# A four-layer transformer kernel: the DMA of the softmax shift rows moves from SyncE's queue to ScalarE's, and the planned order is laid out anew

## The chip, the cores and the metric

The kernel runs on one core of one Trainium2 chip. The time is device microseconds of one execution, from launch to end. Before the change it is 3052.14 us, the median of 3 runs (3050.81 to 3057.52).

## What is computed

Sixteen sequences of 256 tokens with 256 features pass through four transformer layers with 16 heads of 16 features. Seven attentions come out of it: numbers 0, 2 and 4 are self attentions over 256 keys (0 and 2 causal, 4 with a mask), numbers 1, 3, 5 and 6 are cross attentions over a context of 77 rows. Layers 0 and 2 have a dense feed-forward part, layer 1 has a mixture of eight experts with two experts per token, layer 3 is a cross attention alone. Each attention is, in short:

```
q, k, v = x @ wq + bq, ctx @ wk + bk, ctx @ wv + bv       # 16 heads of 16
scores  = q @ k.T / sqrt(16)                              # masked where causal or padded
out     = softmax(scores) @ v @ wo + bo
x       = layernorm(x + out) * gain + bias
```

## The kernel before

The program has three phases. Phase "a" runs layer 0 and both attentions of layer 1 for all 16 sequences and scatters the tokens to their experts; phase "b" runs the experts in 39 groups; phase "c" gathers the experts' outputs and runs layers 2 and 3. In phases a and c up to seven sequences are in flight at once (LANES, line 45).

Nobody writes the instruction order by hand. Functions such as attend_steps (line 317) describe each piece of work as a step: its engine, its booked duration (us), how long after it its result can be used (lag), the steps that it comes after, and the buffers that it takes and gives. Plan.run (line 93) simulates the engines with these figures: whichever step can start first goes next, and among equals the more urgent. Urgency is the length of the way to the end, shifted by hand-fitted amounts for each stage in the table AHEAD (line 446). The result is one fixed list of steps per engine. The engine programs (tensor_program at 683, scalar_program at 916, sync_program at 1404 and so on) go through these lists and emit real instructions with waits on semaphores. In the real run each engine keeps its listed order, and an instruction that has to wait holds up all that is behind it on its engine or queue.

Scores are computed in a split form. Query and key values are split into three bfloat16 parts (high, middle and low, lines 940 to 951 and 1366), and SyncE copies these by DMA into stacks of six blocks of 16 partitions, "qs" for queries and "ks" for keys (copy steps, line 1430, each copy 128 KB for 256 tokens). TensorE multiplies the stacks once with queries as rows (qm steps, line 736); VectorE takes each row's maximum (line 1106) and turns it into a negative shift in three bfloat16 parts. TensorE transposes these (turn_shift, line 744), ScalarE copies them out of PSUM into the tile "shift", of 48 partitions by 256 (turned_shift, line 955), and a DMA of 24 KB puts them as three more partitions under the query stack (shift_in, line 1433, issued by SyncE). Only then can TensorE multiply the stacks again with keys as rows and the shift included (km steps, line 756, opened by the mask matmul of line 865 or 869 in self attention). ScalarE takes the exponential (exp, line 962), and TensorE multiplies with the values (pv, line 772).

There are 64 shift_in steps in phase a and 48 in phase c. The step is booked as 0.76 us of SyncE plus a lag of 2.2 us, which Plan.run multiplies by 1.35 in these phases. The shift tile is one of two buffers; ScalarE waits at line 954 until the DMA that last read it has landed.

Of the kernel before, what the change touches and what calls it, by code (L numbers as in the profile page):

```python
# [22 lines left out]
NPART = 3  # L23
STACK = 6 * HD
# [292 lines left out]
def attend_steps(plan, b, at, qs, ks, values, stacked):  # L317
    causal, n = at in CAUSAL, S if at in SELF else C
    lab = (b, at)
    maxima = ("maxima", lab)  # L320
    units = query_units(at)
    for u, (cost, _, _) in enumerate(units):
# [13 lines left out]
              bank=bank, least=least)  # L336
    plan.step("scalar", "turned_shift", b, at, us=0.41, after=[("turn_shift", b, at)], takes=["shift"], gives=["bank"],
              bank=bank, shift=shift)
    plan.step("sync", "shift_in", b, at, us=0.76, lag=2.2, after=[("turned_shift", b, at)], gives=["shift"], landing="shift",
              shift=shift, qs=qs)  # L340
    flat = ("flat", lab)
    for g in range(H // 4):
# [80 lines left out]
def start_steps(plan, loads):  # L423
# [8 lines left out]
    for at in (0, 1, 2, 3):  # L432
# [10 lines left out]
          "outs": ("out", "add"), "ffs": ("ff", "relu"), "gains": ("bias", "gain", "shift")}  # L443
STAGE_OF = {kind: stage for stage, kinds in STAGES.items() for kind in kinds}
NORM_OF = {"l0_1": 0, "l0_2": 1, "l0_3": "l0_ff", "l1_0": 2, "l1_1": 3, "l1_3": 4, "l2_1": 5, "l2_2": "l2_ff", "l2_3": 6}
AHEAD = {"a": {"enters": 0.9, ("enters", "a"): -0.6, "norms": 3.3, ("norms", 0): 126.0, ("gains", 0): -19.1,
               "turns": -0.8, ("turns", 0): 2.0, "projs": 0.8, ("projs", 0): 13.1, "values": -0.4,
               ("values", 0): 1.0, ("maxima", 0): 0.1, "shifts": 0.2, ("shifts", 0): 69.6, "scores": 0.1,
               ("scores", 0): -0.1, "pvs": -1.3, ("pvs", 0): 0.9, "ends": 0.3, ("ends", 0): 43.8,
               ("enters", 1): -1.6, ("projs", 1): -1.3, ("values", 1): -0.2, "outs": -0.8, ("outs", 0): 0.3,  # L450
               ("norms", 1): 15.5, ("gains", 1): -0.2, ("turns", 1): 9.5, ("maxima", 1): -0.1, ("shifts", 1): 132.0,
               ("scores", 1): 0.1, ("pvs", 1): 230.3, ("ends", 1): -0.4, ("outs", 1): 34.4,
               ("norms", "l0_ff"): -0.5, ("gains", "l0_ff"): 16.9, "ffs": -0.4, ("ffs", "l0_ff"): 1.3,
               ("outs", "l0_ff"): 0.1, ("gains", 2): 20.1, ("projs", 2): -0.1, ("shifts", 2): 1.0,
               ("scores", 2): 0.3, ("pvs", 2): 1.6, ("ends", 2): 0.2, ("enters", 3): -0.6, ("projs", 3): -0.3,
               ("outs", 2): 152.6, ("norms", 3): 74.0, ("turns", 3): -0.1, ("maxima", 3): 1.6, ("shifts", 3): 0.6,
               ("pvs", 3): 1.3, ("ends", 3): -0.8, ("outs", 3): -0.1, ("norms", "l1_2"): -0.5,
               ("turns", "l1_2"): 0.2, ("gains", "l1_2"): 1.8},
         "c": {"enters": 2.3, "norms": 8.4, ("norms", 4): -9.6, "turns": 1.2, ("turns", 4): -0.2, "gains": 4.7,
               ("gains", 4): 30.5, "projs": 0.7, ("projs", 4): -0.5, "values": -0.4, ("values", 4): 1.4,  # L460
               "maxima": -0.2, "shifts": 102.7, ("shifts", 4): 20.1, "scores": 0.2, ("scores", 4): 28.6,
               "pvs": -0.2, ("pvs", 4): 0.1, "ends": -0.1, ("ends", 4): -48.7, ("enters", 5): 2.2,
               ("projs", 5): 67.2, ("values", 5): 15.0, "outs": -1.0, ("outs", 4): 0.4, ("norms", 5): -269.4,
               ("turns", 5): 2.9, ("gains", 5): -88.8, ("maxima", 5): -0.3, ("shifts", 5): 86.2,
               ("scores", 5): -0.5, ("pvs", 5): 16.5, ("ends", 5): 11.0, ("outs", 5): 9.0, ("norms", "l2_ff"): -4.7,
               ("turns", "l2_ff"): 18.2, ("gains", "l2_ff"): 5.1, "ffs": 36.7, ("ffs", "l2_ff"): 30.1,
               ("outs", "l2_ff"): 38.3, ("enters", 6): 1.1, ("projs", 6): 77.4, ("values", 6): 121.8,
               ("norms", 6): 4.9, ("turns", 6): -1.6, ("gains", 6): 4.8, ("shifts", 6): 2.8, ("scores", 6): 19.9,
               ("pvs", 6): 129.6, ("ends", 6): -12.2, ("outs", 6): 29.6, ("norms", "l3"): -8.7,
               ("gains", "l3"): 14.4}}  # L470


def ahead_of(phase):
# [442 lines left out]
def scalar_program(act, k, phase):  # L916
# [4 lines left out]
    for s in k.plan.order[phase]["scalar"]:  # L921
# [18 lines left out]
        elif s.kind == "high":  # L940
            bank, parts, n = tile(s, "bank"), tile(s, "parts"), C if s.part == "c" else S
            bias = k.biases[at][0 if s.part == "q" else 1]
            until.wait_ge(*done("proj", b, at, s.part))
            until.wait_ge(*freed(s, "parts"))
            for m in range(KT):
                ins = act.activation(parts[:, 0, m, 0:n], bank[:, 0, m * n:(m + 1) * n], ACT.Identity, bias=bias[:, m:m + 1])
            ins.then_inc(k.own(s), 1)
        elif s.kind == "middle":
            parts, rest, n = tile(s, "parts"), tile(s, "rest"), C if s.part == "c" else S
            until.wait_ge(*done("rest", b, at, s.part))  # L950
            act.activation(parts[:, 1, :, 0:n], rest[:, :, 0:n], ACT.Copy).then_inc(k.own(s), 1)  # L951
        elif s.kind == "turned_shift":
            until.wait_ge(*done("turn_shift", b, at))
            until.wait_ge(*freed(s, "shift"))
            act.activation(tile(s, "shift"), tile(s, "bank")[0:NPART * H, 0, 0:S], ACT.Copy).then_inc(k.own(s), 1)
        elif s.kind == "exp":
            bank, prob, (g, u) = tile(s, "bank"), tile(s, "prob"), s.part
            rows, (_, _, (first, cols)) = C if at in CROSS else P, key_units(at, g)[u]
            until.wait_ge(*done("km", b, at, s.part))
            if u == 0:  # L960
                until.wait_ge(*freed(s, "prob"))
            act.activation(prob[0:rows, first:first + cols], bank[0:rows, 0, 0:cols], ACT.Exp, scale=SCALE).then_inc(k.own(s), 1)  # L962
        elif s.kind == "value":
            bank, values = tile(s, "bank"), tile(s, "values")
            keys, n = (P, QT) if at in SELF else (C, 1)
            until.wait_ge(*done("value_proj", b, at))
            until.wait_ge(*freed(s, "values"))
            act.activation(values[0:keys, 0:n, 0:H, 0:HD],
                           bank[0:keys, 0, 0:n * D].rearrange("p (t h d) -> p t h d", h=H, d=HD), ACT.Copy).then_inc(k.own(s), 1)
        elif s.kind == "relu":  # L970
            bank, hidden = tile(s, "bank"), as_hidden(tile(s, "hidden"))
            until.wait_ge(*done("ff", b, at, s.part))
            if s.part == 0:
                until.wait_ge(*freed(s, "hidden"))
            for j in range(2):
                f = 2 * s.part + j
                ins = act.activation(hidden[:, f, :], bank[:, 0, j * S:(j + 1) * S], ACT.Relu, bias=k.ff[at][2][:, f:f + 1])
            ins.then_inc(k.own(s), 1)
        elif s.kind == "gelu":
            bank, hidden, b1 = tile(s, "bank"), tile(s, "hidden"), tile(s, "b1")  # L980
            until.wait_ge(*done("expert", b, "b", s.part))
            until.wait_ge(*done("b1_load", b, "b"))
            if s.part == 0:
                until.wait_ge(*freed(s, "hidden"))
            n = ROWS_OF[b]
            per_bank = 2 * S // n
            for j in range(per_bank):
                f = per_bank * s.part + j
                ins = act.activation(hidden[:, f, 0:n], bank[:, 0, j * n:(j + 1) * n], ACT.Gelu, bias=b1[:, f:f + 1])  # L989
            ins.then_inc(k.own(s), 1)  # L990
        elif s.kind == "route_exp":
            r = tile(s, "r")
            until.wait_ge(*done("logit_less", b, at))
            act.activation(r["prob"], r["logit"], ACT.Exp).then_inc(k.own(s), 1)
        elif s.kind == "gap_exp":
            r = tile(s, "r")
            until.wait_ge(*done("gap", b, at))
            act.activation(r["e2"], r["gap"], ACT.Exp).then_inc(k.own(s), 1)
        elif s.kind == "group_store":
            n, slot = ROWS_OF[b], SLOTS[b]  # L1000
            first = slot * GROUP if slot < PAIRS else PAIRS * GROUP + (slot - PAIRS) * HALF
            until.wait_ge(*done("group_sum", b, "b"))
            act.dma_start(rows_of(k.sorted_flat, slice(first, first + n)), tile(s, "y")[:, 0:n // P, :]).then_inc(k.own(s), 16)
        else:
            raise ValueError(s.kind)
# [398 lines left out]
def sync_program(sp, k, phase):  # L1404
# [3 lines left out]
    for s in k.plan.order[phase]["sync"]:  # L1408
# [10 lines left out]
        elif s.kind == "copy":  # L1419
# [8 lines left out]
                until.wait_ge(*done("low", b, at, role))  # L1428
            for block in COPIES[role == "q"][part]:
                sp.dma_start(stack[block * HD:(block + 1) * HD, :, :], parts[:, part, :, 0:n]).then_inc(k.own(s), 16)  # L1430
        elif s.kind == "shift_in":
            until.wait_ge(*done("turned_shift", b, at))
            sp.dma_start(tile(s, "qs")[STACK:STACK + NPART, :, :], tile(s, "shift")).then_inc(k.own(s), 16)
        elif s.kind == "clear":
            rows = lambda first, n: (k.sorted_in[first, :].rearrange("(q p) d -> p q d", p=P),
                                     k.zeros.unsqueeze(1).broadcast_to([P, n // P, D]))
# [368 lines left out]
```

## Time and profile before

| | us |
|---|---|
| median of 3 runs | 3052.14 |
| lowest and highest | 3050.81, 3057.52 |
| the profiled execution, whole | 3048.22 |
| its span, first to last instruction | 3045.8 |
| TensorE busy, share of the span | 2830.4, 93% |
| VectorE busy | 1681.8, 55% |
| ScalarE busy | 1331.7, 44% |
| GpSimd busy | 986.7, 32% |

Phase a goes from the start to about 1410 us, phase b from about 1424 to 1951, phase c from there to the end. Instructions that only issue a DMA are not counted as busy; they stand in the timeline with a q behind the engine's name (SPq, ACTq). "idle before <-releaser" is the time that an engine stood still before an instruction and what ended it. The mean granted TensorE clock over the span is 0.964 of full speed.

### The profile page before, as it was taken

To read this page: it belongs to the slowest core of one execution; us is meant where nothing else is said; L and a number is where in the kernel's file an instruction comes from. 1 tells how busy PE (TensorE), PEld (TensorE's weight loads), DVE (VectorE), ACT (ScalarE), POOL (GpSimd) and SP (SyncE) were. 2 spreads that over 40 slices of the span, in tenths; PEclk is the share of its full clock that TensorE was granted. 3 is DMA by queue.
4 is the path that set the end of the run, shared out by engine and by line. 5 is a ranking of instruction groups with operands and counts; after the bars stand their busy time and mean duration, and the time that the engine had idled before them with its cause. 6 is when DMAs were issued, how large, how long until landed. Compare 5 with 4: busy or idle time off the path is not lost. (4 is left out here: it accounts for less than half of the span.)

```text
span 3045.8 us, 58500 instructions
## 1 busy us (share of the span) xinstructions
PE 2830.4 (93%) x22574; PEld 2279.3 (75%) x22574; DVE 1681.8 (55%) x4086; ACT 1331.7 (44%) x2955; POOL 986.7 (32%) x1103
## 2 busy tenths in 40 slices
PE   6989999989999989975999999889999999999996
PEld 4768888768888777754888888656777777777774
DVE  4646556776755867554110010276676766767664
ACT  2535445556455455332222222245455545555442
POOL 2313224444323444322000000252344444444343
PEclk8999999999999999986999999899999999999997
DMA  9755546585664674754767766375466555666342
GB/s 141 119 72 67 63 54 89 84 114 75 75 71 59 90 98 72 190 74 135 241 225 231 224 211 220 87 111 63 53 85 76 80 79 75 82 77 78 43 50 40
DMA packets 393627, 317.68 MB, mean 104 GB/s; under 512 B 152155, under 2 KB 377307, under 8 KB 393339
## 3 DMA queue, kind: packets, MB, share of 16 engines
q1 hardware_dynamic: 370994, 276.25, 54.6%
q0 software_dynamic: 8272, 23.73, 2.8%
q10 hardware_dynamic: 14085, 13.97, 1.7%
q8 instruction: 179, 2.93, 0.5%
q14 instruction: 97, 0.79, 0.1%
HBM read 133.54 MB, written 36.57 MB: 56 GB/s over the span
## 5 line engine op out<-in xcount | busy, mean ns | idle before, releaser
L962 ACT ACTIVATE a_prob<-a_bank 128x512 f32<-128x512 f32 (+1 forms) x640 | 332.8, 603 | 146.5 <-PE a_bank L756 142.9
L1106 DVE TENSOR_REDUCE a_maxima<-a_bank 128x2 f32<-128x512 f32 (+3 forms) x576 | 339.2, 644 | 82.7 <-PE a_bank L736 82.0
L962 ACT ACTIVATE c_prob<-c_bank 128x512 f32<-128x512 f32 (+1 forms) x512 | 266.3, 599 | 194.7 <-PE c_bank L756 194.4
L989 ACT ACTIVATE b_group_hidden<-b_bank,b_b 128x256 f32<-128x256 f32 (+1 forms) x312 | 123.3, 452 | 387.7 <-PE b_bank L820 387.7
L1106 DVE TENSOR_REDUCE c_maxima<-c_bank 128x6 f32<-128x462 f32 (+1 forms) x448 | 260.4, 635 | 45.2 <-PE c_bank L736 43.9
L865 PE MATMUL a_bank<-a_causal_b,keep_identb 128*128 128x256 bf16 (+1 forms) x768 | 243.1, 316 | 29.9 <-DMA a_qs<-a_shift 12.9
L820 PE MATMUL b_bank<-b_group_xt,b_w 128*128 128x256 f32 (+1 forms) x1248 | 261.6, 364 | 6.3 <-DVE b_group_xt L1157 6.3
L802 PE MATMUL b_bank<-b_w,b_group_hidden 128*128 128x256 f32 x1136 | 251.7, 380 | 0.9 <-ACT b_group_hidden L989 0.9
L820 PEld LDWEIGHTS b_bank<-b_group_xt,b_w 128*128 128x128 f32 x1248 | 220.6, 192 | 33.7 <-DVE b_group_xt L1157 8.3
L802 PEld LDWEIGHTS b_bank<-b_w,b_group_hidden 128*128 128x128 f32 x1136 | 215.6, 190 | 29.7 <-ACT b_group_hidden L989 1.3
L1163 DVE TENSOR_TENSOR b_group_y<-b_bank,b_b 128x512 f32<-128x512 f32 (+1 forms) x39 | 25.1, 644 | 336.1 <-PE b_bank L802 336.1
L1359 POOL TENSOR_TENSOR c_tok<-c_tok,weights_row_L_xattn_ln_g 128x512 f32<-128x512 f32 x64 | 81.2, 1268 | 192.9 <-PE c_bank L705 192.7
L756 PE MATMUL a_bank<-a_qs,a_ks 99*128 99x128 bf16 x1536 | 143.5, 222 | 0.0
L736 PE MATMUL a_bank<-a_ks,a_qs 96*128 96x128 bf16 x1536 | 142.4, 220 | 0.0
L756 PEld LDWEIGHTS a_bank<-a_qs,a_ks 99*128 99x128 bf16 x1536 | 121.6, 99 | 22.9 <-issue 1.4
L736 PEld LDWEIGHTS a_bank<-a_ks,a_qs 96*128 96x128 bf16 x1536 | 120.2, 98 | 23.6 <-issue 2.2
L1132 DVE STREAM_TRANSPOSE a_flat<-a_bank 128x512 f32<-128x512 f32 x128 | 90.0, 708 | 86.5 <-PE a_bank L772 86.0
L714 PE MATMUL a_bank<-a_xt,a_at_q 128*128 128x256 f32 x512 | 131.8, 404 | 5.7 <-ACT a_xt L935 4.4
L802 PE MATMUL a_bank<-a_at_o,a_heads 128*128 128x256 f32 x512 | 131.3, 402 | 5.6 <-DVE a_heads L1140 5.4
L1152 DVE TENSOR_TENSOR a_tok<-a_bank,a_tok 128x512 f32<-128x512 f32 x80 | 54.8, 687 | 146.3 <-PE a_bank L802 146.0
L1369 POOL TENSOR_TENSOR a_parts_q<-a_rest,a_parts_q 128x512 bf16<-128x512 f32 x64 | 74.0, 1158 | 183.0 <-ACT a_parts_q L951 183.0
L1386 POOL DMA_INDIRECT c_pair_y<-sorted_out,keep_rows x64 | 62.8, 982 | 200.7 <-issue 195.1
(255 smaller groups left out, 6224.0 us busy)
## 6 DMA issues: line engine op xcount, KB each, us to landing
b_w<-in_L_xattn_e_w SPq DMA_DIRECT2D x78, 1024.0 KB, 7.4
a_qs<-a_parts_q SPq DMA_DIRECT2D x384, 128.0 KB
c_qs<-c_parts_q SPq DMA_DIRECT2D x288, 128.0 KB
a_ks<-a_parts_k SPq DMA_DIRECT2D x192, 128.0 KB, 5.9
c_ks<-c_parts_k SPq DMA_DIRECT2D x96, 128.0 KB, 5.5
sorted_in<-a_zeros SPq DMA_DIRECT2D x8, 1024.0 KB
b_group_x<-sorted_in SPq DMA_DIRECT2D x32, 256.0 KB, 6.8
sorted_out<-b_group_y ACTq DMA_DIRECT2D x32, 256.0 KB, 4.8
```

The costliest lines, as they stand in the source:

```text
L714: ins = pe.matmul(bank[:, 0, m * n:(m + 1) * n], weight[:, kt, m * P:(m + 1) * P], xt[:, kt, 0:n], start=(kt == 0), stop=(kt == KT - 1))
L736: ins = pe.matmul(bank[:, 0, to:to + m], qs[0:STACK, h, q * P:(q + 1) * P], ks[0:STACK, h, kt * P:kt * P + m], start=(at in CROSS), stop=( ...
L756: ins = pe.matmul(bank[0:kn, 0, to:to + m], ks[0:STACK + NPART, h, kt * P:kt * P + kn], qs[0:STACK + NPART, h, q0:q0 + m], start=(at in CR ...
L802: ins = pe.matmul(bank[:, 0, q * D:(q + 1) * D], heads[:, kt, q * P:(q + 1) * P], weight[:, kt, :], start=(kt == 0), stop=(kt == kts - 1))
L820: ins = pe.matmul(bank[:, 0, j * n:(j + 1) * n], weight[:, kt, f * P:(f + 1) * P], xt[:, kt, 0:n], start=(kt == 0), stop=(kt == KT - 1))
L865: pe.matmul(blocks, k.identb, k.causal[:, keys_first, :].unsqueeze(1).broadcast_to([P, 4 // step, P]), start=True, stop=False)
L962: act.activation(prob[0:rows, first:first + cols], bank[0:rows, 0, 0:cols], ACT.Exp, scale=SCALE).then_inc(k.own(s), 1)
L989: ins = act.activation(hidden[:, f, 0:n], bank[:, 0, j * n:(j + 1) * n], ACT.Gelu, bias=b1[:, f:f + 1])
L1106: v.tensor_reduce(maxima[:, q:q + qn, h:h + n].rearrange("p q h -> p h q"), bank[:, 0, 0:cols].rearrange("p (j q n) -> p j q n", j=n, q=qn ...
L1132: v.transpose(flat, tile(s, "bank")[:, 0, :].rearrange("p (g b c) -> p g b c", g=2, c=32)).then_inc(k.own(s), 1)
L1359: pool.tensor_tensor(x, x, over(k.gains[at][0]), ALU.mult).then_inc(k.own(s), 1)
L1369: pool.tensor_tensor(parts[:, 2, :, 0:n], rest[:, :, 0:n], parts[:, 1, :, 0:n], ALU.subtract).then_inc(k.own(s), 1)
```

## The change

The step shift_in is planned and issued on ScalarE, with 0.1 us booked where SyncE had 0.76. ScalarE waits for the end of its own copy and then issues the same DMA with the same semaphore. The table AHEAD has new values in both phases, so the planned order of all engines is laid out anew. Nothing that is computed changes.

```diff
-    plan.step("sync", "shift_in", b, at, us=0.76, lag=2.2, after=[("turned_shift", b, at)], gives=["shift"], landing="shift",
+    plan.step("scalar", "shift_in", b, at, us=0.1, lag=2.2, after=[("turned_shift", b, at)], gives=["shift"], landing="shift",
               shift=shift, qs=qs)
...
-AHEAD = {"a": {"enters": 0.9, ("enters", "a"): -0.6, "norms": 3.3, ("norms", 0): 126.0, ("gains", 0): -19.1,
...
+AHEAD = {"a": {"enters": 0.9, ("enters", "a"): -2.7, "norms": 1.6, ("norms", 0): 201.3, "gains": -7.4,
...
             act.activation(tile(s, "shift"), tile(s, "bank")[0:NPART * H, 0, 0:S], ACT.Copy).then_inc(k.own(s), 1)
+        elif s.kind == "shift_in":
+            until.wait_ge(*done("turned_shift", b, at))
+            act.dma_start(tile(s, "qs")[STACK:STACK + NPART, :, :], tile(s, "shift")).then_inc(k.own(s), 16)
...
-        elif s.kind == "shift_in":
-            until.wait_ge(*done("turned_shift", b, at))
-            sp.dma_start(tile(s, "qs")[STACK:STACK + NPART, :, :], tile(s, "shift")).then_inc(k.own(s), 16)
```

## Rows read from the trace of the kernel before

**Rows 1.** The page: busy us, share of the span, instructions of each engine.
```profile
PE 2830.4 (93%) x22574; PEld 2279.3 (75%) x22574; DVE 1681.8 (55%) x4086; ACT 1331.7 (44%) x2955; POOL 986.7 (32%) x1103
```

**Rows 2.** By stretch: length, busy of PE, PEld, DVE, ACT, POOL; clock; DMA share; GB/s.
```profile
1350.00:1450.00 100.00, 61.66 (x361) 47.34 (x360) 44.87 (x171) 22.32 (x49) 31.90 (x34) 0.68 0.47 133
2060.00:2800.00 740.00, 717.50 (x5676) 542.47 (x5675) 500.83 (x1147) 383.01 (x833) 321.26 (x355) 1.00 0.59 75
2950.00:3046.00 96.00, 69.58 (x485) 53.01 (x483) 45.59 (x106) 29.20 (x64) 32.70 (x37) 0.78 0.20 35
```

**Rows 3.** Waits of TensorE (us, times, longest); the first is the same for 2060 to 2800.
```profile
PE c_bank L869 <- DMA c_qs<-c_shift: 20.9, 13, 3.5
PE a_bank L865 <- DMA a_qs<-a_shift: 12.9, 6, 5.9
PE a_bank L865 <- DMA a_qs<-a_parts_q: 10.7, 3, 7.7
PE a_bank L756 <- DMA a_qs<-a_shift: 9.4, 6, 3.6
PE a_bank L714 <- ACT a_xt L935: 4.4, 4, 1.1
PE c_bank L756 <- DMA c_qs<-c_shift: 2.0, 2, 1.8
```

**Rows 4.** SyncE's timeline, the chain (start, us, what), TensorE's timeline, at 2521 to 2537.
```profile
2520.98 1.89 SPq L1430 DMA_DIRECT2D c_qs<-c_parts_q  x3
...
2531.14 5.61 DMA c_qs<-c_shift
...
2536.80 0.39 PE L869 MATMUL c_bank<-c_weights_mask_k,keep_identb 128*128 128x512 bf16 x1 [0.88 <-DMA c_qs<-c_shift]
```

**Rows 5.** Timeline of SyncE and TensorE at 1369 to 1373.
```profile
1369.69 0.77 SPq L1433 DMA_DIRECT2D a_qs<-a_shift  x1
1372.47 1.29 PE L756 MATMUL a_bank<-a_qs,a_ctx_ks 99*77 99x256 bf16 x5 [1.14 <-DMA a_qs<-a_shift]
```

**Rows 6.** Timeline of ScalarE and SyncE at 1261 to 1270.
```profile
1261.61 0.37 ACT L955 ACTIVATE a_shift<-a_bank 48x256 bf16<-48x256 f32 x1
1268.31 1.99 SPq L1433 DMA_DIRECT2D a_qs<-a_shift  x1
```

**Rows 7.** Instructions of line 1433: duration ns min/median/max, first and last start.
```profile
L1433 SPq DMA_DIRECT2D c_qs<-c_shift x48: 737/767/784, 2012.7 to 3014.7; - x48
```

**Rows 8.** Waits of SyncE's queue: total us, times, longest us.
```profile
SPq L1433 <- ACT c_shift L955: 297.0, 42, 15.9
```

**Rows 9.** DMA issues of the expert phase: count, KB each, median us to landing.
```profile
b_group_x<-sorted_in SPq DMA_DIRECT2D x32, 256.0 KB, 6.8
sorted_out<-b_group_y ACTq DMA_DIRECT2D x32, 256.0 KB, 4.8
```

**Rows 10.** Issues of the ones rows on ScalarE (line 925) and SyncE (1412).
```profile
L925 ACTq DMA_DIRECT2D a_ctx_ks<-in_ones_b x3: 716/720/865, 1.6 to 3.3; - x3
L1412 SPq DMA_DIRECT2D c_ctx_ks<-in_ones_b x2: 731/792/852, 1952.0 to 1952.9; - x2
```

**Rows 11.** Timeline of ScalarE behind three shift copies, and one row of TensorE.
```profile
2532.52 0.84 ACT L946 ACTIVATE c_parts_q<-c_bank,keep_columns 128x256 bf16<-128x256 f32 x2 [1.41 <-PE c_bank L714]
...
2554.20 0.84 ACT L946 ACTIVATE c_parts_q<-c_bank,keep_columns 128x256 bf16<-128x256 f32 x2 [1.30 <-PE c_bank L714]
...
2579.25 0.38 ACT L968 ACTIVATE c_ctx_values<-c_bank 77x256 f32<-77x256 f32 x1 [0.50 <-PE c_bank L723]
2579.69 1.02 ACT L935 ACTIVATE c_xt<-c_bank,keep_columns 128x256 f32<-128x256 f32 x2
2580.80 1.96 PE L714 MATMUL c_bank<-c_xt,c_weights_at_q 128*128 128x256 f32 x8
```

**Rows 12.** Timeline of ScalarE at a shift copy of phase a.
```profile
487.16 0.37 ACT L955 ACTIVATE a_shift<-a_bank 48x256 bf16<-48x256 f32 x1
487.42 3.94 ACT L962 ACTIVATE a_prob<-a_bank 77x512 f32<-77x512 f32 x8
```

More of the change, by code:

```diff
@@ L445 @@
 NORM_OF = {"l0_1": 0, "l0_2": 1, "l0_3": "l0_ff", "l1_0": 2, "l1_1": 3, "l1_3": 4, "l2_1": 5, "l2_2": "l2_ff", "l2_3": 6}
-AHEAD = {"a": {"enters": 0.9, ("enters", "a"): -0.6, "norms": 3.3, ("norms", 0): 126.0, ("gains", 0): -19.1,
[L447 to L470, printed above, removed]
@@ new lines @@
+AHEAD = {"a": {"enters": 0.9, ("enters", "a"): -2.7, "norms": 1.6, ("norms", 0): 201.3, "gains": -7.4,
+               ("gains", 0): 65.6, ("turns", 0): -0.4, "projs": 0.8, ("projs", 0): 35.2, "values": -0.3,
+               ("values", 0): 0.3, ("maxima", 0): 11.1, "shifts": 1.1, ("shifts", 0): 88.2, "scores": 0.1,
+               ("scores", 0): -0.8, "pvs": -1.3, ("pvs", 0): 0.3, "ends": 1.7, ("ends", 0): 121.4,
+               ("enters", 1): 17.2, ("projs", 1): -1.4, ("values", 1): -1.2, "outs": -1.5, ("outs", 0): 1.3,
+               ("norms", 1): 51.4, ("gains", 1): -4.6, ("turns", 1): 57.5, ("shifts", 1): 25.3, ("scores", 1): 0.1,
+               ("pvs", 1): 336.2, ("ends", 1): -1.3, ("outs", 1): 44.9, ("norms", "l0_ff"): 10.2,
+               ("gains", "l0_ff"): 53.9, ("turns", "l0_ff"): -0.5, "ffs": -0.2, ("outs", "l0_ff"): -28.8,
+               ("turns", 2): 93.3, ("values", 2): 3.3, ("maxima", 2): 0.3, ("shifts", 2): 125.4, ("scores", 2): 0.3,
+               ("pvs", 2): -99.3, ("ends", 2): -39.3, ("enters", 3): -4.6, ("values", 3): 2.1, ("outs", 2): 163.5,
+               ("norms", 3): 84.9, ("turns", 3): -0.1, ("gains", 3): 14.8, ("shifts", 3): 2.7, ("pvs", 3): 0.9,
+               ("ends", 3): -5.1, ("outs", 3): 0.2, ("norms", "l1_2"): -0.5, ("turns", "l1_2"): 0.6,
+               ("gains", "l1_2"): 23.0},
+         "c": {"enters": 16.0, ("enters", "c"): -4.4, "norms": 123.0, ("norms", 4): -0.3, "turns": 0.5,
+               ("turns", 4): -0.9, "gains": -37.5, ("gains", 4): 6.6, "projs": 32.9, ("projs", 4): 9.0,
+               "values": -1.6, ("values", 4): 2.4, "maxima": -0.2, "shifts": 425.5, ("shifts", 4): -3.8,
+               "scores": -16.5, ("scores", 4): 220.9, "pvs": -14.9, ("pvs", 4): 54.2, "ends": -77.9,
+               ("ends", 4): 1.2, ("enters", 5): 3.3, ("projs", 5): 74.2, ("values", 5): 107.5, "outs": -1.2,
+               ("outs", 4): 0.4, ("norms", 5): -397.8, ("turns", 5): 69.3, ("gains", 5): -47.6, ("maxima", 5): -0.1,
+               ("scores", 5): 37.9, ("pvs", 5): 241.4, ("ends", 5): 160.2, ("outs", 5): 245.1,
+               ("norms", "l2_ff"): 14.3, ("turns", "l2_ff"): 88.8, "ffs": 65.1, ("ffs", "l2_ff"): -11.4,
+               ("outs", "l2_ff"): 47.3, ("enters", 6): 2.4, ("projs", 6): 107.5, ("values", 6): 132.2,
+               ("norms", 6): -7.9, ("turns", 6): 0.8, ("gains", 6): 7.2, ("shifts", 6): 2.7, ("scores", 6): 58.8,
+               ("pvs", 6): 47.1, ("ends", 6): -0.5, ("outs", 6): 57.1, ("norms", "l3"): -3.2,
+               ("gains", "l3"): -21.4}}
```

## The prediction

> **What bounds the kernel now.** I read the page's busy table first: TensorE is busy 2830.4 of 3045.8 us, ScalarE 1331.7 [rows 1]. So the end is set by TensorE's work plus its idle time, 3045.8 − 2830.4 = 215 us, and an edit that leaves TensorE's work alone can only move that idle time. The table by stretch then says where it lies: from 2060 to 2800 only 22.5 us are lost, but 38.3 us in the hundred at 1350 and 26.4 us in the last 96 [rows 2]. In the steady stretch the granted clock is 1.00, the upper of the two levels (2.4 GHz), so nothing is to be had there from the clock. The waits of TensorE name the causes: the landing of the shift rows costs 20.9 + 12.9 + 9.4 + 2.0 = 45.2 us, in 13 + 6 + 6 + 2 = 27 waits, the copies of query parts 10.7 us, and the largest wait for ScalarE 4.4 us in all [rows 3]. The 20.9 us lie all between 2060 and 2800 and are nearly the whole of the 22.5 [rows 2, 3]. The change aims at the largest single wait of the steady stretch.
>
> Next, why that wait is there. In the pattern that recurs every 63 us, SyncE issues 12 copies back to back from 2520.98 on, and behind them the shift rows at 2531.14; the chain shows 5.61 us to the landing, and TensorE stands 0.88 us [rows 4]. Where nothing has been issued for a while (1369.69) TensorE starts on the shift at 1372.47, so that landing took 2.7 us [rows 5]. The transfer is the same, so about 3 us of the landing are what stands before it in SyncE's queue. And at 1261.98 the copy on ScalarE ends, but SyncE issues the rows only at 1268.31 [rows 6], behind clears and stack copies of its own; that is the longest wait, 5.9 us [rows 3].
>
> **The change part by part.** *The issue leaves SyncE.* 64 + 48 = 112 issues of 0.77 us, 86 us of SyncE [rows 7], and, more important, the waits in which SyncE stood with a shift issue at its head, in the last phase alone 297.0 us [rows 8]. Copies behind it can go earlier. Of the 10.7 us of waits for copies I take nothing back for that: 7.7 us is a single wait [rows 3]. Bounds 0 and −11.
>
> *The landing gets shorter.* On ScalarE's queue nothing stands ahead of the rows in the two attention phases, apart from the first loads. No row of the kernel before shows this transfer on that queue while copies run. Nearest rows: the empty case, 2.7 us [rows 5], and the 256 KB store from ScalarE's queue in the expert phase, beside SyncE's loads, 4.8 us against 6.8 for a load of that size from SyncE [rows 9]. The rows are 24 KB, a tenth, so I take the middle of 2.7 and 4.8, some 3.8 us; the bounds are 2.7 and the present 5.6. The cover that TensorE's order gives is landing less wait, 5.61 − 0.88 = 4.7 us [rows 4]; at 3.8 us that wait is gone. Over the 27 waits this leaves, by my estimate, some 5 us: where the landing is at 2.7 already (the 1.14 us at 1372.47, [rows 5]) or the cover is under 3.8. Gain 45 − 5 = 40 us; with the landing unchanged it is 0.
>
> The Trainium skill speaks on both sides here ("DMA: Bandwidth & Descriptors"). Against, in "SWDGE vs HWDGE vs iDMA": transfers of all issuing engines run on the same 16 DMA engines, and another issuer saves only issue time. By it the landing would stay near 6 us and the 40 us would be 0. For, in "Queues, rings and completion order": each DMA engine takes turns between the queues it has work for, by packets; by that the rows pass the copies. That ScalarE's store lands before SyncE's load would [rows 9] agrees rather with the second.
>
> *The issue lands on ScalarE.* The planner books 0.1 us for it. Its real price: loads of the ones rows, also to three partitions, take 720 ns on ScalarE and 792 on SyncE at the median [rows 10], so the issuer matters little, and I take SyncE's 0.77 us for the shift [rows 7]. ScalarE must first wait for the end of its own copy, which loses the overlap of 0.1 us seen at 487.16 + 0.37 against 487.42 [rows 12]. So 0.87 us each, 112 × 0.87 = 97 us. ScalarE is busy 383.0 of 740 us in the steady stretch [rows 2], so most of it lies beside TensorE's work. Queued behind it are exp, the parts' high and middle, the turned tokens and the values; pv, projections and free banks on TensorE wait for these. Three shift copies make up a sequence of the last phase. Behind the first (2531) ScalarE idles 1.41 us: no cost. Behind the second (2552) comes one exp, then 1.30 us idle: no cost. Behind the third (2578) the values begin 0.50 us later, the turned tokens end at 2580.71, and TensorE's projection on them begins at 2580.80 [rows 11]; pushed by 0.87 − 0.50 = 0.37 us, with 0.1 us of slack, TensorE loses 0.3 us. One in three loses 0.3: 112 × 0.1 = 11 us. In the first phase a run of eight exps without a gap [rows 12] passes the whole push on, and the new order counts on 0.1 us, so I take half as much again: 16 us lost. Bounds 0 and 97.
>
> *The order.* The steps' priorities are new, so TensorE's own order changes in both phases. Its work does not: the same matmuls. What can move is the idle time at the starts and ends of the phases, such as the 38.3 and 26.4 us [rows 2]. No row says which way; I take 0, and ±12 us, a fifth of those 65.
>
> **Sum.** The profiled execution took 3048.2 us, of which 3045.8 are span; the median of three runs is 3052.1, so 4 us above. −40 + 16 + 0 = −24: profiled 3024, median 3028 us.
>
> **Rivals.** *1. ScalarE passes the price on.* The order books 0.1 us where 0.77 is real, and puts dependent work close behind. It decides from the point where more than 40/0.87 = 46 of the 112 issues reach TensorE in full. For it: the exps without a gap [rows 12]. Against: ScalarE is half idle [rows 2], and its longest wait in rows 3 is 1.1 us. With two thirds, 3052 − 40 + 65 = 3077; with all, 3109. Slower. *2. The landing does not shorten*, because the 16 DMA engines, busy 0.59 of the stretch [rows 2], are the same for both queues: gain 0, cost 11 to 16, so 3063 to 3068. Slower; the first rule of the Trainium skill above is this case. Against: the 4.8 us [rows 9]. *3. The waits go but the time comes back*, at the next late thing or at the phase ends of a changed order (twice the ±12 above): 3046 to 3058, no change. *4. The change does not do what it says*: if the planner sets other ScalarE steps between the copy and the issue, the rows start later by an exp or more, 0.5 us each (3.94 us for eight, [rows 12]); with 2 us on most waits half the gain is gone, 3046 to 3050, no change.
>
> **How the numbers follow.** A measurement of this kernel tells about 0.2%, 6 us, from no change. Forecast (below 3046): 0.62, of which 0.05 lies under 3000. Rivals 3 and 4: 0.16. Rival 2: 0.08. Rival 1: 0.14, a third of it under 3068. The range 3000 to 3068 leaves out the 0.05 below and two thirds of rival 1, 0.09, above. The forecast's own range: landing gain 30 to 45, ScalarE 5 to 30, order ±12 give about 3000 to 3046. Faster 0.62, same 0.16, slower 0.22.
>
> **What would show it.** TensorE's waits for the shift landing fall from 45 us to under 10. The shift lands about 3.8 us after its issue on ScalarE beside copies (rival 2: 6). The issue takes 0.77 us there, and TensorE's waits for ScalarE grow by some 16 us (rival 1: over 40). SyncE's waits for the shift copy vanish. TensorE's busy time stays at 2830 ± 5 and the steady clock at 1.00. The prediction is wrong if the idle time at the phase ends moves by more than 12 us, or if TensorE's busy time moves.

## The result and the profile after

| | us |
|---|---|
| kernel before, median of 4 runs (lowest to highest) | 3051.47 (3048.48 to 3057.52) |
| kernel after, median of 4 runs (lowest to highest) | 3142.71 (3141.66 to 3144.36) |
| after / before, 95% interval | 1.0297 (1.0279 to 1.0315) |

The change makes the kernel 3.0% slower, 91 us. The forecast was 3028 us, faster; the range ended at 3068. In the code of after, every line from 956 on stands 3 lower than in before (the issue on ScalarE is L958, the exp L965, the stack copies stay L1433).

The page of after: span and busy times; they answer to [rows 1].

```profile
span 3140.9 us, 58466 instructions
...
PE 2857.0 (91%) x22492; PEld 2288.4 (73%) x22574; DVE 1675.9 (53%) x4086; ACT 1336.2 (43%) x2955; POOL 986.6 (31%) x1103
```

The span grew by 3140.9 − 3045.8 = 95.1 us. TensorE is busy 2857.0 − 2830.4 = 26.6 us more and idle (3140.9 − 2857.0) − 215.4 = 68.5 us more. 82 matmul records are missing from this trace (22492 against 22574); at the mean of 2857.0 / 22492 = 0.127 us some 10 us of the idle time are in truth busy time, so the split is rather 58 and 37. The matmuls are the same, so the busy time can only have grown by slower ones. Where the time went is told by the same stretches in both kernels. First phase a, from the start; then phase c in three pieces, cut at its first norm, at the second and the tenth store of its results, and at the last. Columns: length; busy of PE, PEld, DVE, ACT, POOL; clock; DMA share; GB/s. Before:

```profile
0.00:1397.00 1397.00, 1288.00 (x12095) 1049.57 (x12096) 889.30 (x2260) 676.37 (x1483) 479.17 (x536) 0.96 0.61 88
1962.80:2302.10 339.30, 313.61 (x2359) 227.76 (x2362) 226.23 (x500) 164.60 (x349) 146.90 (x160) 0.96 0.63 80
2302.10:2811.18 509.08, 496.11 (x3960) 378.36 (x3956) 353.29 (x816) 263.64 (x577) 238.45 (x265) 1.00 0.60 78
2811.18:3040.30 229.12, 205.14 (x1578) 159.23 (x1570) 134.87 (x306) 99.01 (x223) 84.33 (x96) 0.92 0.35 47
```

After:

```profile
0.00:1434.00 1434.00, 1301.79 (x12096) 1048.97 (x12097) 887.90 (x2260) 678.84 (x1483) 479.52 (x536) 0.96 0.60 86
1998.90:2359.20 360.30, 317.32 (x2327) 229.99 (x2359) 223.10 (x502) 165.17 (x353) 146.08 (x160) 0.94 0.60 76
2359.20:2892.50 533.30, 502.58 (x3904) 383.81 (x3944) 358.74 (x816) 265.41 (x576) 237.64 (x264) 0.97 0.61 75
2892.50:3135.40 242.90, 210.70 (x1586) 163.26 (x1590) 128.74 (x308) 99.98 (x223) 85.87 (x98) 0.92 0.31 44
```

Phase a is 37 us longer, the ramp of phase c 21, its steady part 24, its drain 14; phase b is not longer. Read the clock of the steady part: 1.00 before, 0.97 after. TensorE's busy time there is 6.5 us more in the rows, and with the 56 missing records at 0.127 us some 14. As much, 13.8 us, is phase a's, where the clock is 0.96 in both rows.

TensorE's waits of after (total us, times, longest); the rows on the shift answer to [rows 3].

```profile
PE c_bank L756 <- DMA c_qs<-c_shift: 51.0, 15, 10.0
PE a_bank L756 <- DMA a_qs<-a_shift: 20.1, 8, 5.0
...
PE a_bank L865 <- DMA a_qs<-a_parts_q: 17.5, 6, 9.2
...
PE a_bank L744 <- DVE a_least_parts L1128: 11.6, 8, 3.9
...
PE c_bank L714 <- ACT c_xt L935: 7.1, 5, 2.9
PE a_bank L865 <- DMA a_qs<-a_shift: 6.5, 4, 2.5
```

The waits for the shift, which were to fall from 45.2 us to under 10, rose to 51.0 + 20.1 + 6.5 = 77.6 us. The issue and the chain of after say why; these rows answer to [rows 7] and [rows 4].

```profile
L958 ACTq DMA_DIRECT2D c_qs<-c_shift x48: 728/729/764, 2052.9 to 3109.7; - x48
```

```profile
2467.37 7.87 DMA c_qs<-c_shift
...
2535.62 7.81 DMA c_qs<-c_shift
```

The issue costs what was thought, 0.73 us. But the rows, alone on ScalarE's queue, take 7.8 us to land, where they took 5.61 us behind twelve copies on SyncE's queue. Over all of the steady part the chains have ten such landings in after, 7.1 to 8.0 us, and nine in before, 5.6 to 7.1 with a median of 6.35: the row of [rows 4] is the shortest of them. SyncE's timeline of after around 2535 us shows what is under way meanwhile:

```profile
2525.92 1.86 SPq L1433 DMA_DIRECT2D c_qs<-c_parts_q  x3
...
2527.86 4.13 SPq L1433 DMA_DIRECT2D c_ks<-c_parts_k  x5
...
2532.04 1.25 SPq L1433 DMA_DIRECT2D c_qs<-c_parts_q  x2
...
2533.63 0.55 SPq L1433 DMA_DIRECT2D c_ks<-c_parts_k  x1
...
2534.23 0.59 SPq L1433 DMA_DIRECT2D c_qs<-c_parts_q  x1
...
2534.93 3.23 SPq L1433 DMA_DIRECT2D c_ctx_ks<-c_parts_k  x5
```

SyncE issues copies with hardly a gap from 2525.92 to 2538.16. Twelve of 128 KB go out in 8.9 us, where before took 10.2 us for its twelve [rows 4], and five smaller ones, of 38.5 KB, follow; ScalarE's 24 KB goes out at 2535.62, behind the twelve and the first of the five.

### The profile page after: what moved, and what is told of

It reads as the page before. It is cut to its first block and busy times, and to the rows that moved or that the text cites. A ratio compares the mean times of both kernels' runs of the same rounds, so it can differ in the third digit from the quotient of the medians.

```text
span 3140.9 us, 58466 instructions
## 1 busy us (share of the span) xinstructions
PE 2857.0 (91%) x22492; PEld 2288.4 (73%) x22574; DVE 1675.9 (53%) x4086; ACT 1336.2 (43%) x2955; POOL 986.6 (31%) x1103
## 5 line engine op out<-in xcount | busy, mean ns | idle before, releaser
L965 ACT ACTIVATE a_prob<-a_bank 128x512 f32<-128x512 f32 (+1 forms) x640 | 334.1, 605 | 180.8 <-PE a_bank L756 167.8
L965 ACT ACTIVATE c_prob<-c_bank 128x512 f32<-128x512 f32 (+1 forms) x512 | 265.4, 604 | 186.3 <-PE c_bank L756 184.5
L1109 DVE TENSOR_REDUCE c_maxima<-c_bank 128x6 f32<-128x462 f32 (+2 forms) x448 | 263.3, 635 | 53.1 <-PE c_bank L736 52.7
L865 PE MATMUL a_bank<-a_causal_b,keep_identb 128*128 128x256 bf16 (+1 forms) x768 | 247.8, 323 | 38.2 <-DMA a_qs<-a_parts_q 17.5
L756 PE MATMUL c_bank<-c_qs,c_ks 99*128 99x256 bf16 x512 | 104.7, 287 | 47.5 <-DMA c_qs<-c_shift 42.3
L756 PE MATMUL a_bank<-a_qs,a_ks 99*128 99x128 bf16 x1536 | 144.1, 222 | 0.0
L756 PEld LDWEIGHTS a_bank<-a_qs,a_ks 99*128 99x128 bf16 x1536 | 121.6, 99 | 23.2 <-issue 1.6
```

Of the source, the lines that this page charges most:

```text
L756: ins = pe.matmul(bank[0:kn, 0, to:to + m], ks[0:STACK + NPART, h, kt * P:kt * P + kn], qs[0:STACK + NPART, h, q0:q0 + m], start=(at in CR ...
L865: pe.matmul(blocks, k.identb, k.causal[:, keys_first, :].unsqueeze(1).broadcast_to([P, 4 // step, P]), start=True, stop=False)
L1109: v.tensor_reduce(maxima[:, q:q + qn, h:h + n].rearrange("p q h -> p h q"), bank[:, 0, 0:cols].rearrange("p (j q n) -> p j q n", j=n, q=qn ...
```

## The experiments

The theory after the first look: **T1**, the landing depends on the copies issued before it, from whichever queue, and the new order puts more of them before the rows; the order loses the time, the queue is nearly indifferent. Rivals: **T2**, ScalarE's issue and its wait are what costs; **T3**, the new order is longer by its own dependencies, backlog or not. Times are medians; each ratio is against the kernel before on the same chip, since that kernel's median itself was 3073.7 us on the chip of e1, e2, e3 and e5 and 3049.7 to 3050.5 on the others. There is no trace of the kernel before from the slower chip, so a row of e1 or e2 beside one of before compares two chips as well.

### e1 and e2: queue alone, order alone

e1 keeps the order of before and lets ScalarE send the rows right behind its copy:

```diff
             act.activation(tile(s, "shift"), tile(s, "bank")[0:NPART * H, 0, 0:S], ACT.Copy).then_inc(k.own(s), 1)
+            until.wait_ge(*done("turned_shift", b, at))
+            send = k.plan.steps["shift_in", b, at, 0]
+            act.dma_start(tile(send, "qs")[STACK:STACK + NPART, :, :], tile(send, "shift")).then_inc(k.own(send), 16)
...
-            until.wait_ge(*done("turned_shift", b, at))
-            sp.dma_start(tile(s, "qs")[STACK:STACK + NPART, :, :], tile(s, "shift")).then_inc(k.own(s), 16)
+            pass
```

> The planned order of the kernel before on every engine, to the letter; only the issue of the shift rows moves: ScalarE sends them right behind its copy. Theory O (the loss comes from the newly laid out order, the queue itself helps or is neutral): 3020 to 3055 us, waits of TensorE on the shift landing 45 us or less. Theory Q (the loss comes from the queue: ScalarE's issue time and a landing that is no shorter): 3100 to 3150 us, most of the 91 us. In the last phase the landing of the shift issued near 2531 us tells whether ScalarE's queue passes the copies: 3.8 us if it does, 5.6 to 6.3 us if it does not.

e2 takes the order of after and lets SyncE send, at the place in its list that the planned start of the step gives:

```diff
+        sends = [s for s in order.get("scalar", []) if s.kind == "shift_in"]
+        order["sync"] = sorted(order["sync"] + sends, key=at_time)
...
-            until.wait_ge(*done("turned_shift", b, at))
-            act.dma_start(tile(s, "qs")[STACK:STACK + NPART, :, :], tile(s, "shift")).then_inc(k.own(s), 16)
+            pass
```

> The order of the changed kernel on every engine, but SyncE sends the shift rows, at the place in its list where the plan has the step in time. Theory O: 3110 to 3150 us, near the changed kernel, with a period of about 68 us per sequence in the last phase and a clock of 0.95 there. Theory Q: 3045 to 3070 us.

| | us | ratio to before (95%) |
|---|---|---|
| e1, queue alone | 3066.8 | 0.9975 (0.9960 to 0.9991) |
| e2, order alone | 3187.0 | 1.0370 (1.0343 to 1.0396) |

The order does all of the harm and the queue a little good. In the new order the queue brings somewhat more (from 1.0370 to 1.0297) than in the old one. T2 falls with this: e2, which issues nothing on ScalarE, is slower than after. On the scale where before takes 3052 us e1 is at 3044, inside what its order theory expected, and e2 at 3165, above the 3110 to 3150 expected. The chain of e1 first, then that of e2: start, us, the landing on which TensorE waited.

```profile
2485.00 6.04 DMA c_qs<-c_shift
...
2548.31 6.13 DMA c_qs<-c_shift
```

```profile
2427.78 7.73 DMA c_qs<-c_shift
...
2496.49 7.67 DMA c_qs<-c_shift
```

These are all four cases. Over the steady part, in the old order the landing takes 5.6 to 7.1 us from SyncE (before) and 5.9 to 7.0 from ScalarE (e1); in the new order 6.8 to 7.8 from SyncE (e2) and 7.1 to 8.0 from ScalarE (after). The queue doesn't shorten it. TensorE's waits of e1:

```profile
PE c_bank L756 <- DMA c_qs<-c_shift: 21.1, 12, 2.6
...
PE a_bank L865 <- DMA a_qs<-a_parts_q: 18.5, 5, 15.2
...
PE a_bank L756 <- DMA a_qs<-a_shift: 3.2, 3, 1.4
...
PE a_bank L865 <- DMA a_qs<-a_shift: 2.1, 2, 1.6
```

In phase c the wait is as before (21.1 against 20.9 + 2.0 us), with the copies still in front. In phase a, where SyncE could come late to the issue [rows 6], it falls from 12.9 + 9.4 us to 3.2 + 2.1. Part of that comes back in one longer wait for the query parts (18.5 us against 10.7). That e1's small gain is this difference fits these rows; it isn't shown by itself.

### e3: the new issue with the old priorities

The kernel after with the table AHEAD of before.

```diff
-AHEAD = {"a": {"enters": 0.9, ("enters", "a"): -2.7, "norms": 1.6, ("norms", 0): 201.3, "gains": -7.4,
...
+AHEAD = {"a": {"enters": 0.9, ("enters", "a"): -0.6, "norms": 3.3, ("norms", 0): 126.0, ("gains", 0): -19.1,
...
```

> The changed kernel with the old priority table: step moved and booked at 0.1 us on ScalarE, order planned anew from the old numbers. If any order that the planner makes from these bookings is as good as another (the small-change view of the prediction, plus or minus 12 us), 3010 to 3060 us. If an order is only as good as the fit of the table to exactly these bookings (theory O), well over the changed kernel: the planner's own end of the phases is 59 us later in the first and 94 us later in the last phase than for the kernel before, so 3180 to 3300 us.

3299.9 us, 1.0735 (1.0712 to 1.0758). The two parts of the diff can't be judged apart by swapping the table: it is fitted to the booked times, and with 0.1 us booked for the shift in place of 0.76 it lays out an order that loses 226 us. By its ratio that is 3276 us where before takes 3052, inside the 3180 to 3300 expected. This run separates nothing between T1 and T3; it shows only how much hangs on the fit of the table to the booked times, and that "order 0 ± 12 us" had no ground.

### e5: more issues on ScalarE

The kernel before, with one DMA more on ScalarE behind each shift copy (48 rows of a constant to spare DRAM), its result used by nobody.

```diff
+            until.wait_ge(*done("turned_shift", b, at))
+            act.dma_start(k.spare_rows[k.spare_sent], k.identb[0:NPART * H, :]).then_inc(k.sem("spare"), 16)
+            k.spare_sent += 1
```

> The kernel before, with SyncE still sending the shift rows, and an extra DMA issue of the same form on ScalarE behind each shift copy (48 rows of 256 bytes from a constant to spare rows in device memory; nothing else reads them). It measures what 112 issues cost on ScalarE alone. Forecast's term: 11 us, 3055 to 3070 us. Rival 1: half or more of 97 us, 3100 to 3150 us.

3080.4 us, 1.0022 (1.0010 to 1.0034): the 112 waits and issues cost 6.7 us in all, 0.06 us each, at the low end of what was expected. But they are shorter than the issue that they stand for:

```profile
L958 ACTq DMA_DIRECT2D spare_rows<-keep_identb x112: 308/309/386, 60.7 to 3047.7; - x112
```

The shift issue takes 0.73 us on ScalarE, this one 0.31, so 6.7 us is less than the price of the real one. e11 below gives that price.

### e6 and e7: both kernels with a smaller backlog

From the sixth sequence on, each copy of key parts to the stack moves one eighth of its bytes, in after (e6) and in before (e7). The attention of these sequences is therefore not that of the reference; the instructions and their order are as they were. The key copies of the first five sequences and all query copies keep their size. The edit of either:

```diff
-                sp.dma_start(stack[block * HD:(block + 1) * HD, :, :], parts[:, part, :, 0:n]).then_inc(k.own(s), 16)
+                if role == "q" or b < 5:
+                    sp.dma_start(stack[block * HD:(block + 1) * HD, :, :], parts[:, part, :, 0:n]).then_inc(k.own(s), 16)
+                else:
+                    sp.dma_start(stack[block * HD:(block + 1) * HD, 0:KT, :], parts[0:P:P // HD, part, :, 0:n]).then_inc(k.own(s), 16)
```

> The changed kernel, but from the sixth sequence on each copy of key parts into the key stack moves only the first two heads (an eighth of the bytes, the same number of issues; the rest of the stack keeps older data, so attention is not computed as in the reference). Theory B (a backlog of copies in the DMA engines, ahead of the shift rows on whichever queue they are sent, makes the landing long; TensorE's stall then also costs clock): the landing in the recurring pattern falls from 7.8 us to 3 to 5 us, the stall from 3.5 us to under 1 us, the granted clock there from 0.95 to 1.00 and the period from 68.2 to 62 to 64 us, so 3060 to 3095 us. Rival P (the new order itself holds TensorE up by its dependencies, whatever the DMAs do): period stays over 66 us, 3120 to 3140 us.

> The same cut in the kernel before (SyncE sends the shift rows; from the sixth sequence on key copies move an eighth of the bytes). Theory B: landing of the shift behind the copies falls from 6.2 us to 3 to 4.5 us, its waits in the last phase from 20.9 us to under 8, period 63.3 to about 62 us; 3025 to 3040 us on the scale where the kernel before takes 3052, so the distance between the two kernels shrinks from 91 us to 30 to 60. Rival P: the distance stays near 90 us.

| | us | ratio to before (95%) |
|---|---|---|
| e6, new order, short key copies | 3047.2 | 0.9984 (0.9967 to 1.0001) |
| e7, old order, short key copies | 2991.1 | 0.9805 (0.9786 to 0.9824) |

The bytes taken away cost the new order 3142.7 − 3047.2 = 95.5 us and the old one some 3049.7 − 2991.1 = 58.6 us. Both runs came out faster than expected, the distance between them within the 30 to 60 us expected. So the new order loses 37 us more to these bytes, and 3047.2 − 2991.1 = 56 us of the loss stay. T1 is right in kind and explains two fifths. For the rest T3 is likely but not shown: the ramps of both phases are those of the first five sequences, whose copies are whole. TensorE's waits for the shift are 26.0 us in e6 and 21.9 in e7, so the long landing itself is little of the 56. The steady part of phase c, from 2400 to 2800 us, in after, e6 and e7, in this order:

```profile
2400.00:2800.00 400.00, 376.38 (x2890) 286.80 (x2924) 265.67 (x603) 197.58 (x427) 178.02 (x198) 0.97 0.60 74
```

```profile
2400.00:2800.00 400.00, 399.05 (x3195) 303.96 (x3193) 289.95 (x663) 216.48 (x471) 193.20 (x215) 1.00 0.39 63
```

```profile
2400.00:2800.00 400.00, 399.90 (x3172) 305.39 (x3171) 284.55 (x657) 210.85 (x462) 184.08 (x206) 1.00 0.32 58
```

With short copies TensorE loses at most 1 us of 400 in either order, and the clock of the new order is back at 1.00. In the steady part, then, backlog and clock are nearly the whole loss. The 56 us lie elsewhere, as the norms of phase c (line 1084 in e6, 1081 in e7; count, duration ns, first and last start) show, e6 first:

```profile
L1084 DVE BATCH_NORM_AGGREGATE c_moments<-c_stats x160: 138/150/183, 1954.8 to 3038.5; 128x2 f32<-128x6 f32 x160
```

```profile
L1081 DVE BATCH_NORM_AGGREGATE c_moments<-c_stats x160: 123/152/183, 1928.8 to 2980.0; 128x2 f32<-128x6 f32 x160
```

Phase c begins 26 us later, so that much was lost before it, in phase a if phase b is again no longer; from first to last norm it takes 1083.7 against 1051.2 us, 32 more, with a steady part as quick: ramp and drain. What the time went into, by the sums of all rows of e6 against e7: waits for VectorE 78.0 against 69.8 us, for ScalarE 25.0 against 16.6, for the query parts 11.1 against 2.9, for the shift 26.0 against 21.9, and busy time 2845.2 against 2824.0 for the same 22574 matmuls.

### e8: the rows on GpSimd's queue

The order of before, the issue merged into GpSimd's list at its planned time.

```diff
+        sends = [s for s in order["sync"] if s.kind == "shift_in"]
+        order["gpsimd"] = sorted(order["gpsimd"] + sends, key=at_time)
...
+            pool.dma_start(tile(s, "qs")[STACK:STACK + NPART, :, :], tile(s, "shift")).then_inc(k.own(s), 16)
```

> The order of the kernel before on the other engines; GpSimd sends the shift rows, at the place in its list where the plan has the step in time. It tells whether any queue passes the backlog. Theory B1 (one line of descriptors for SyncE and ScalarE, none for GpSimd's queue): landing in the recurring pattern well under 6 us from the start of the data, though GpSimd takes about 1 us to issue and stands in its own order; 3040 to 3080 us. Theory B2 (the 16 DMA engines are simply full): landing 6 us or more, 3060 to 3120 us.

3075.5 us, 1.0086 (1.0054 to 1.0117), from two runs. Its chain shows a third queue with the same landing, 5.0 to 6.9 us over the steady part (median 6.56), so not the short one of its theory B1. Why the kernel is 0.9% slower than before is open.

```profile
2547.56 6.54 DMA c_qs<-c_shift
```

### e9: hold the copies back, on SyncE's queue

If what counts is what was issued just before, the cure is not another queue but another place in the same one. e9 is the kernel before. After planning, each shift issue in SyncE's list is moved ahead of the stack copies in front of it, as long as such a copy started at most 5 us before it in the plan and its first reader starts over 7.5 us after it, plus 0.65 us for each issue passed.

```diff
+            while (first and queue[first - 1].kind == "copy" and begun[key(queue[first - 1])] > at - window
+                   and needed[key(queue[first - 1])] > at + landing + 0.65 * (i - first)):
+                first -= 1
+            moved += i - first
+            queue[first:i + 1] = [s] + queue[first:i]
```

> The kernel before; only SyncE's list is rearranged: each issue of shift rows is moved ahead of stack copies planned in the 5 us before it, where the plan leaves these copies at least 7.5 us more than they need (162 places moved in all). SyncE then holds those copies until the shift rows are on their way; the computation is whole. Theory B (the backlog of copies ahead of the shift rows makes their landing long): in the recurring pattern the landing falls from 6.2 us to about 3 us, the waits on it from 45 us to under 20, the period from 63.3 to about 61.7 us; 3015 to 3040 us against 3052. Rival H (holding the copies only moves the wait to them): waits for stack copies grow by as much as the shift's fall, 3045 to 3070 us.

3012.5 us, 0.9863 (0.9830 to 0.9897): 38 us faster than before, 130 faster than after, with the whole computation, and just below the range expected. (The rule passes 110 copies, 52 of them in phase a, and not the 162 of the expectation.) SyncE's and TensorE's timeline of e9:

```profile
2442.80 0.76 SPq L1460 DMA_DIRECT2D c_qs<-c_shift  x1
2443.60 1.45 SPq L1457 DMA_DIRECT2D c_ks<-c_parts_k  x2
...
2447.64 0.39 PE L783 MATMUL c_bank<-c_qs,c_ks 99*128 99x256 bf16 x2
```

(Lines of e9 from TensorE's on stand 27 higher: L783 is L756, L892 is L865.) The copies now start behind the rows, and the first matmul on the rows starts 4.8 us after their issue without a wait. That bounds the landing from above; the 3 us expected can't be read, since nothing waited for it. TensorE's waits of e9 for the shift:

```profile
PE a_bank L892 <- DMA a_qs<-a_shift: 6.7, 2, 5.8
...
PE a_bank L783 <- DMA a_qs<-a_shift: 1.6, 2, 1.1
...
PE c_bank L783 <- DMA c_qs<-c_shift: 0.6, 1, 0.6
```

8.9 us of the 45.2 are left. This is the gain that the prediction computed, 36 us of waits and 38 us of time, got by another means: the place in the queue, not another queue. That waits for the copies would grow by as much (rival H) didn't happen: those for the parts are 16.8 us in all rows, against 13.8 before.

### e10 and e11: the same rule in the new order, and with ScalarE's queue

e10 is e2 with the rule of e9. e11 is e1 with the rule of e9.

```diff
-        self.order[phase] = order
+        self.order[phase] = self.shifts_first(order, begun, needs) if phase != "b" else order
```

> The same rearrangement of SyncE's list in the order of the changed kernel, with SyncE sending the shift rows (so it is to be held against order alone, 1.037 of the kernel before). Theory B: the recurring period falls from 68.6 us to 62 to 63, the granted clock there from 0.95 to 1.00; 1.005 to 1.02 of the kernel before. Rival P (the order itself is slow): 1.03 or more.

> The rearranged list of SyncE in the order of the kernel before, but ScalarE sends the shift rows; SyncE only waits for ScalarE's copy at that place and then goes on with the held copies. With the backlog gone from both, it tells what ScalarE's queue itself is worth. Theory B: the queue gives no shorter landing and costs ScalarE's issue time (ratio 1.002 measured for it), and spares SyncE 0.77 us each: within 0.3% of the run with the shift first, so 0.984 to 0.990 of the kernel before. If ScalarE's queue had a merit of its own in the landing: 0.980 or less.

| | us | ratio to before (95%) |
|---|---|---|
| e10, new order, SyncE, copies held | 3092.3 | 1.0121 (1.0093 to 1.0149) |
| e11, old order, ScalarE, copies held | 3028.7 | 0.9930 (0.9914 to 0.9945) |

In the new order the rule brings 1.0370 down to 1.0121, as expected, but the new order still stands 3092.3 − 3012.5 = 80 us above the old one. That isn't the order without the backlog either. TensorE's waits of e10 for the shift:

```profile
PE c_bank L786 <- DMA c_qs<-c_shift: 26.2, 13, 10.4
PE a_bank L786 <- DMA a_qs<-a_shift: 20.7, 6, 6.7
PE a_bank L895 <- DMA a_qs<-a_shift: 16.1, 2, 15.8
```

63.0 us of them are left, where e9 has 8.9, and in its steady part the landing still takes 6.6 to 7.8 us. So up to 54 of the 80 us are waits for the shift that the rule did not take away. One period of e10's steady part, then one of e9's:

```profile
2411.51:2474.02 62.51, 61.15 (x488) 46.97 (x493) 44.74 (x102) 33.29 (x72) 29.75 (x34) 1.00 0.65 80
```

```profile
2403.79:2465.42 61.63, 61.19 (x496) 47.23 (x498) 44.21 (x102) 32.98 (x73) 29.86 (x33) 1.00 0.62 81
```

The period is 0.9 us longer, where after's eight periods were 24.2 / 8 = 3.0 us longer each, and the clock is 1.00. Again the rest is at the ends. In the old order, with the rows no longer waiting, ScalarE's queue is a loss: e11 is 16 us slower than e9 by the medians, more than expected (0.984 to 0.990); by the two intervals it is 5 us at least. In its trace the shift waits are down as well, but the one for the query parts stands at 18.2 us where e9 has 10.7:

```profile
PE a_bank L892 <- DMA a_qs<-a_parts_q: 18.2, 4, 15.4
```

All rows of waits for ScalarE together are 23.6 us against 16.4 in e9. These 7.5 and 7.2 us make 15 of the 16. The same wait of 15 us was in e1. This is the price of the real issue of 0.73 us where the landing has nothing left to gain: 16 us for 112, 0.14 us each.

## Why the prediction was wrong

**What bounds the kernel: right.** The shift waits of 45.2 us were the largest thing to be had; e9 took 36 us of them and the kernel became 38 us faster. That some 3 us of the landing are what had been issued before it was right too, by e9; the row read for it, 5.61 us [rows 4], is the shortest of nine, whose median is 6.35.

**"The landing gets shorter", −40 us: this step failed.** It held the copies to be in the way because they stood ahead *in the same queue*. Over the steady part e1 shows 5.9 to 7.0 us on ScalarE's queue, e8 5.0 to 6.9 on GpSimd's, against 5.6 to 7.1 on SyncE's; in after, where 3.8 us was forecast, it is 7.1 to 8.0. The nearest row chosen, the 256 KB store at 4.8 us [rows 9], was a poor one: it doesn't tell what was under way beside the store, and the landing hangs on that. The Trainium skill's rule in "DMA: Bandwidth & Descriptors", section "SWDGE vs HWDGE vs iDMA", that all issuers share the 16 engines, is what these landings bear out. The rule of the same page in "Queues, rings and completion order", that an engine takes turns between queues, didn't help these rows: on a queue of their own they gained nothing. The gain that e1 does have, 8 us of time by its ratio, probably came from the other effect, the issue that no longer waits for its turn in SyncE's list: phase a's waits fell by some 17 us. The prediction had named that effect [rows 6] and given it no term.

**"The issue lands on ScalarE", +16 us: borne out.** One issue takes 0.73 us as expected, and e11 against e9 puts the whole at 16 us by the medians, with wide intervals. That it fits to the microsecond is luck: the sum of one issue in three at 0.3 us was not tested, and half of the 16 us came by way of the query parts, which it doesn't hold. In after, all rows of TensorE's waits for ScalarE grew from 14.8 to 28.8 us, as much as forecast; but e2, with no issue on ScalarE, has 30.9, so that growth belongs to the order. The 40 us of rival 1 aren't there.

**"The order", 0 ± 12 us: this step failed, and it is the large one.** e2 measures it as +3.7%, 113 us, nine times the bound. Two things were missing. The bound was made from the idle time at two places [rows 2], as if an order could only shift what is there; and no thought was given to what a new order does *to the landing*, although that had just been found to hang on the copies in front. Of the 91 us of after, 37 are lost to the backlog and its consequences (e6, e7); the other 56 lie in phase a, in the ramp and in the drain of phase c (e6 against e7). In after as a whole TensorE waits 82.1 us for VectorE in all rows, against 72.2, and 17.5 for the query parts at the opening of self attention in phase a, against 10.7 [rows 3]. Which steps of the order make them late is not settled; no run moved single steps, and none took the whole backlog away.

**The clock: not foreseen.** "Steady clock at 1.00" held for before and fell for after. The stretches behind a stall of 3.58 us in after:

```profile
2407.40:2411.00 3.60, 3.56 (x13) 2.16 (x13) 0.58 (x2) 2.12 (x4) 0.00 (x0) 0.50 1.16 122
2411.00:2414.00 3.00, 3.00 (x14) 2.31 (x13) 0.48 (x1) 0.63 (x2) 0.00 (x0) 0.70 1.00 96
2414.00:2417.00 3.00, 3.00 (x23) 2.01 (x21) 2.52 (x10) 2.19 (x6) 1.46 (x4) 1.00 0.04 9
```

TensorE is busy all of the time from 2407.4 on, but at 0.50 (1.2 GHz) it gets through 13 matmuls in 3.6 us, then 14 in 3.0, where at 1.00 (2.4 GHz) it does 23 (of a somewhat different mix). By the clock, 3.6 × 0.50 + 3.0 × 0.30 = 2.7 us are lost beside the 3.6 of the stall. But not every such stall does this. Two neighbouring periods of after have the same stall, and one of them keeps its clock; the two stalls in TensorE's timeline, and the two periods:

```profile
2612.11 0.64 PE L756 MATMUL c_bank<-c_qs,c_ks 99*128 99x256 bf16 x2 [3.50 <-DMA c_qs<-c_shift]
2680.68 0.38 PE L756 MATMUL c_bank<-c_qs,c_ks 99*128 99x256 bf16 x2 [3.56 <-DMA c_qs<-c_shift]
```

```profile
2563.94:2632.19 68.25, 64.24 (x496) 48.79 (x498) 44.85 (x102) 33.37 (x73) 29.77 (x34) 0.95 0.60 73
2632.19:2698.07 65.88, 61.55 (x496) 47.24 (x498) 44.83 (x102) 33.03 (x73) 29.75 (x34) 1.00 0.62 76
```

The slow clock alone makes the period 2.4 us longer, with as many matmuls in it. Nor is before free of it: behind its stall of 2.33 us the clock is at 0.50 too, behind the one of 2.58 us at 2220.86 it stays at 1.00.

```profile
2600.94 0.39 PE L869 MATMUL c_bank<-c_weights_mask_k,keep_identb 128*128 128x512 bf16 x1 [2.33 <-DMA c_qs<-c_shift]
```

So a stall can cost 2.4 to 2.7 us more than its length, and its length alone doesn't tell which will. Over the eight steady periods a clock of 0.97 is 533 × 0.03 = 16 us, close to the 14 us of busy time more. Of the backlog's 37 us, waits for the shift are some 28: with the short copies they fall from 77.6 to 26.0 us in the new order and from 45.2 to 21.9 in the old one. The slow work behind them was not separated by a run.

**The rivals.** The answer is none of the four. Rival 2's premise held, the landing doesn't shorten; but e1, which is that case in the old order, came out at 0.9975 and not 11 to 16 us slower, and after is 91 us slower. Rival 1 gave 3077 to 3109, on the right side, by a mechanism that e2 excludes: there ScalarE issues nothing, and the time is longer still. Rival 3 was closest in kind, the time coming back at the ends of a changed order, and gave 3046 to 3058.

**What would show it.** Of the signs named, the issue price came as foreseen (0.73 us) and SyncE no longer waits for the shift copy; the landing came out as in rival 2 or worse (7.8 us), shift waits rose, busy time rose by 26.6 us and the steady clock fell to 0.97. The last line, "wrong if the idle time at the phase ends moves by more than 12 us, or if TensorE's busy time moves", named both faults.

## What to carry to other kernels

A short transfer with a deadline is delayed by the long ones *issued just before it*, on whatever queue; before moving it to another queue, move it ahead of the copies that can wait (38 us here, where the other queue brought 8). A new order of a planned kernel is not a term of 0 with a small error: measure it apart from the edit that it comes with, and expect it to change every landing that depends on what is under way. On TensorE a wait can cost more than its length, because the clock may fall behind it. And a stand-in for an issue must take as long as the real one before its price says anything.

## What the runs showed of the hardware

- A 24 KB transfer issued in a run of 128 KB copies lands in 5.0 to 7.1 us from any of three queues (SyncE in before, ScalarE in e1, GpSimd in e8), and in 6.8 to 8.0 in the new order, where the run before it is denser (SyncE in e2, ScalarE in after); with nothing before it, 2.7 us [rows 5].
- Two stalls of TensorE of 3.50 and 3.56 us in the same kernel: the clock fell to 0.50 behind the first and not behind the second, and the period was 68.25 us against 65.88.
- With the landing no shorter, 112 issues of 0.73 us on ScalarE, busy half of the time, in place of SyncE cost the kernel 16 us by the medians (e11 against e9); 112 more issues of 0.31 us cost it 6.7 us (e5).
